# A new prologue, one run of squares and a packed router product in an eight-layer attention kernel with a mixture of experts

## The reference

```
q, k, v = x Wq + bq, x Wk + bk, x Wv + bv
Q, K    = elu(q) + 1, elu(k) + 1
KV, Ks  = sum over the sequence of K*v, of K
V       = Q * KV / (Q * Ks + 1e-6)
x       = layernorm(gelu(V Wo + bo) + x)
x       = layernorm(gelu(gelu(x Wf1 + bf1) Wf2 + bf2) + x)
```

## Time and profile before

| | before |
|---|---|
| median of 3 runs | 1018.92 us (1017.19 to 1019.16) |
| profiled execution | 1018.27 us |
| its span | 1016.2 us |
| PE busy | 952.5 us, 94% |
| DVE busy | 883.3 us, 87% |
| ACT busy | 823.2 us, 81% |
| POOL busy | 108.2 us, 11% |

### The profile page before, as it was taken

The page is one execution under the profiler, slowest core; times in us unless marked ns, Lnnn a source line. Parts: engine busy times, 40 slices in busy tenths (PEclk is TensorE's granted clock), DMA queues, the critical chain, the costliest instruction groups (busy, mean ns, idle before and its releaser), DMA issues.

```text
span 1016.2 us, 13426 instructions
## 1 busy us (share of the span) xinstructions
PE 952.5 (94%) x3621; PEld 606.3 (60%) x3621; DVE 883.3 (87%) x2332; ACT 823.2 (81%) x1334; POOL 108.2 (11%) x109
## 2 busy tenths in 40 slices
PE   5799999999999999999999999999999889999994
PEld 3555555555555555555555555555555567777773
DVE  6768999999999999999999999999998787788875
ACT  4689999999999999999899999999998754444442
POOL 3100000000000000000000000000001122333331
PEclk9999999999999999999999999999999999999997
DMA  9000000000000000020000000000002000000000
GB/s 338 1 0 1 1 0 1 1 1 1 0 1 1 1 0 1 1 83 1 1 1 6 1 1 1 0 1 1 1 0 83 1 1 1 11 11 12 12 21 21
DMA packets 8200, 15.86 MB, mean 16 GB/s; under 512 B 960, under 2 KB 5440, under 8 KB 8000
## 3 DMA queue, kind: packets, MB, share of 16 engines
q1 hardware_dynamic: 7696, 14.82, 4.1%
q10 hardware_dynamic: 432, 0.20, 0.1%
HBM read 12.92 MB, written 2.10 MB: 15 GB/s over the span
## 4 chain that ended last, share of the span: by engine, by line
PE 60%; ACT 15%; DVE 13%; issue 10%; POOL 1%; DMA 1%; SPq 0%; POOLq 0%; DVEq 0%; ACTq 0%
PE Oa L866 11%; PE Ob L866 7%; PE R L764 7%; PE R L766 6%; PE R L765 6%; PE SV L907 4%; ACT L609 4%; PE Ob L821 3%; ACT rs L493 2%; DVE Kt L1425 2%; ACT rz L472 2%; ACT L648 2%; DVE rz L1357 2%; PE Cb L821 1%; PE Ca L886 1%
## 5 line engine op out<-in xcount | busy, mean ns | idle before, releaser
L512 ACT ACTIVATE hid<-R,par 128x512 f32<-128x512 f32 x224 | 148.5, 698 | 14.2 <-PE R L766 12.2
L866 PE MATMUL Oa<-hid,wraw 128*128 128x512 f32 x256 | 133.7, 603 | 1.4
L866 PE MATMUL Ob<-hid,wraw 128*128 128x512 f32 x256 | 130.8, 592 | 0.0
L764 PE MATMUL R<-x_h,wf_h 128*128 128x512 f32 x224 | 105.7, 472 | 0.5 <-ACT hid L512 0.5
L764 PE MATMUL R<-xr_h,wqkv_h 128*128 128x512 f32 x160 | 87.5, 547 | 14.5 <-DVE cen L1685 10.4
L493 ACT ACTIVATE rs<-SV,eps_ln 128x512 f32<-128x512 f32 x128 | 88.4, 690 | 11.7 <-PE SV L907 6.4
L1272 DVE SCALAR_TENSOR_TENSOR y<-x,par,y 128x512 f32<-128x512 f32 x120 | 87.5, 749 | 3.9 <-ACT y L521 3.6
L1283 DVE TENSOR_TENSOR y_l<-y,y_h 128x512 fp32r<-128x512 f32 x128 | 87.8, 686 | 1.2
L765 PE MATMUL R<-x_l,wf_h 128*128 128x512 f32 x224 | 87.9, 392 | 0.0
L766 PE MATMUL R<-x_h,wf_l 128*128 128x512 f32 x224 | 87.9, 392 | 0.0
L498 ACT ACTIVATE rs<-rs 128x512 f32<-128x512 f32 x128 | 80.8, 631 | 1.2
(11 more groups left out here) (249 smaller groups left out, 2400.1 us busy)
## 6 DMA issues: line engine op xcount, KB each, us to landing
wraw<-w_dram SPq DMA_DIRECT2D x7, 768.0 KB, 12.1
x<-x_dram SPq DMA_DIRECT2D x8, 256.0 KB, 6.0
Q<-x_dram SPq DMA_DIRECT2D x1, 2048.0 KB, 7.3
out_dram<-reluq SPq DMA_DIRECT2D x7, 256.0 KB, 2.3
wraw<-w_dram SPq DMA_DIRECT2D x2, 512.0 KB, 5.2
wraw<-w_dram SPq DMA_DIRECT2D x1, 576.0 KB, 6.5
wraw<-row_dram SPq DMA_DIRECT2D x1, 512.0 KB, 5.0
wraw<-bias_dram SPq DMA_DIRECT2D x1, 512.0 KB, 6.1
```

Source lines behind the costliest of these rows:

```text
L512: nc.scalar.activation(hid[:, m * CH:(m + 1) * CH], HIDDEN[m][:, :], GELU, bias=param(u // 4, BF1 + m % FB)).then_inc(hid_done, 1)
L764: nc.tensor.matmul(bank, w_h, a_h, start=True, stop=False)
L866: mm = nc.tensor.matmul(O[h][:, :], raw(u // 4, WF2 + j * P, P), hid[:, m * CH:(m + 1) * CH], start=(j == 0), stop=(j == FB - 1))
```

## The change

It does six things.

1. **Order and banks of the first step.** The prologue becomes a `first_step` on PE, DVE and ACT. K and V of units 0 and 1 come ahead of Q; V alternates between R1 and SV, Q between Oa and Ca, so that each has its own bank. Q's parts of unit 1 lie in `hid`, unused yet. Unit 2's K, V and its first Q are in this step too; its second Q is in step 1; unit 3 moves from step 1 to step 2.
2. **Row copies on three engines.** DVE makes the high part of chunk 0 and the low parts of 0 to 3 and 6, 7; ACT the high parts of 1 to 7 (`split_first`, in step 1 for 6 and 7) and of Wf1; POOL the low parts of 4 and 5 alone.
3. **PE's start.** PE no longer waits for `cen`, whose copy moves behind the first four halves. Ahead of its first product stand 44 unread products of `mean_r` with itself (128x128), into Ob. The fill of 15, and those of 14 in steps 0 and 1, become one of 14 in step 0.
4. **A table load** for exp and log follows the two gelus of step 0 at once.
5. **Router.** The high and low parts of the router weight lie side by side (`rw_parts`): two passes a tile in place of three, 8 and 4 columns wide. DVE adds the two halves with one more reduction, so a chunk's gates have 20 operations (19 before).
6. **Squares.** `squares` of tile 2 and `scale_x` run one after the other, not woven.

On DVE, at the start of the program (xr_h and xr_l are the parts of a chunk, R0 to R2 and SV banks, Kt the product K*V): before,

The diff, cut to its core:

```diff
-            if s < 2:
-                return s + 2
-            return s + 1 if 3 <= s < UNITS - 1 else None
+            return s + 1 if 1 <= s < UNITS - 1 else None
+
+        def q_bank(u, h):
+
+            return (O[0], CB[0])[h] if u < 2 else Q_BANK[h]
+
+        def v_bank(u, h):
+            return (R[1], SV)[h] if u < 2 else V_BANK
+
+        def q_parts(u, h):
+
+            if u == 1:
+                return hid[:, half(h)], hid[:, half(2 + h)]
+            return expq[:, half(h)], reluq[:, half(h)]
...
+            def split_first(c):
+
+                u, h = c // 2, c % 2
+                act.wait_ge(x_loaded[c], 16)
+                after(act, Q_mm, upto(u - 2, h))
+                nc.scalar.activation(xr_h[:, ring(u, h)], x[:, chunk(u, h)], ACT.Copy).then_inc(first_high, 1)
+
+            def high_f_first():
+                act.wait_ge(wfirst_loaded, 16)
+                nc.scalar.activation(wf1_h[0][:, :], raw(0, WF1, FB * P), ACT.Copy).then_inc(wf_high, 1)
+
+            def first_step():
+                exp_k(0, 0)
+                exp_k(0, 1)
+                exp_q(0, 0)
+                relu_q(0, 0)
+                exp_k(1, 0)
+                exp_q(0, 1)
+                relu_q(0, 1)
+                split_first(4)
+                exp_k(1, 1)
+                split_first(5)
+                for h in range(2):
+                    exp_q(1, h)
+                    relu_q(1, h)
+                high_f_first()
+                exp_k(2, 0)
+                exp_k(2, 1)
+                log_z(0)
+                exp_z(0)
+                nc.scalar.preload_act_table_set("gelu_apprx_tanh_and_others")
+                gelu_attend(0, 0)
+                gelu_attend(0, 1)
+                nc.scalar.preload_act_table_set("natural_log_exp_and_others")
+                square(0, 0, 0)
+                high_square(0, 0, 0)
+                square(0, 0, 1)
...
+                if s == 1:
+                    log_z(1)
                 if attends and s % 2 == 1:
                     exp_z(s)
+                if s == 1:
+                    split_first(6)
+                    split_first(7)
...
-            for u in range(2):
-                for h in range(2):
-                    exp_k(u, h)
-                    exp_q(u, h)
-                    relu_q(u, h)
+            for c in range(1, 4):
+                split_first(c)
...
-                    nc.tensor.matmul(SV[:, 0:QKV], cen[:, :], w[:, 0:QKV], start=True, stop=True)
+                    nc.tensor.matmul(O[1][:, 0:w.shape[1]], mean_r[:, :], w, start=True, stop=True)
...
-                    o = O[0][:, t * EXPERTS:(t + 1) * EXPERTS]
-                    nc.tensor.matmul(o, xe_h[:, par_tile(k, t)], rw_h[:, :], start=True, stop=False)
-                    nc.tensor.matmul(o, xe_l[:, par_tile(k, t)], rw_h[:, :], start=False, stop=False)
-                    mm = nc.tensor.matmul(o, xe_h[:, par_tile(k, t)], rw_l[:, :], start=False, stop=True)
+                    both = O[0][:, 2 * t * EXPERTS:2 * (t + 1) * EXPERTS]
+                    nc.tensor.matmul(both, xe_h[:, par_tile(k, t)], rw_parts[:, :], start=True, stop=False)
+                    mm = nc.tensor.matmul(both[:, 0:EXPERTS], xe_l[:, par_tile(k, t)], rw_h, start=False, stop=True)
...
+            def first_step():
+                pe.wait_ge(consts_set, 2)
+                fill(44, mean_r[:, :])
+                for h in range(2):
+                    project(-1, 0, h, "K")
+                    project(-1, 0, h, "V")
+                for h in range(2):
+                    project(-1, 0, h, "Q")
+                    project(-1, 1, h, "K")
+                    project(-1, 1, h, "V")
+                for h in range(2):
+                    project(-1, 1, h, "Q")
+                project(1, 2, 0, "K")
+                project(1, 2, 0, "V")
+                project(1, 2, 1, "K")
+                pe.wait_ge(sums_done, 2)
+                fill(14, wqkv_h[0][:, :])
+                attend_out(0, 0, None)
+                attend_out(0, 1, None)
+                project(1, 2, 1, "V")
+                project(1, 2, 0, "Q")
+                pe.wait_ge(consts_set, 4)
+                pe.wait_ge(reluq_done, upto(1, 1))
+                centre(0, 0, 0)
+                centre(0, 0, 1)
...
-                if s == 0:
-                    fill(15, wqkv_h[0])
                 if p is not None:
                     project(s, p, 1, "Q")
+                if p is not None and s > 1:
                     project(s, p, 1, "V")
...
-                if s == 1:
-                    pe.wait_ge(ln_done[0], upto(0, 1))
-                    pe.wait_ge(wf_set, 1)
-                    fill(14, wf1_h[0])
...
-                if s == 0:
-                    fill(14, wqkv_h[0])
...
+            def high_first():
+
+                dve.wait_ge(x_loaded[0], 16)
+                nc.vector.tensor_copy(xr_h[:, ring(0, 0)], x[:, chunk(0, 0)]).then_inc(chunk0_high, 1)
+
+            def low_first(c):
                 u, h = c // 2, c % 2
-                dve.wait_ge(x_loaded[c], 16)
-                after(dve, kvq_mm, 3 * upto(u - 2, h))
-                nc.vector.tensor_copy(xr_h[:, ring(u, h)], x[:, chunk(u, h)]).then_inc(first_high, 1)
+                if c == 0:
+                    dve.wait_ge(chunk0_high, 1)
+                else:
+                    dve.wait_ge(first_high, c)
+                nc.vector.tensor_tensor(xr_l[:, ring(u, h)], x[:, chunk(u, h)], xr_h[:, ring(u, h)].bitcast(F32),
+                                        ALU.subtract).then_inc(first_low, 1)
...
-                count(nc.vector.tensor_tensor(by_tile(logits[:, :]), by_tile(O[0][:, 0:TE]),
+                parts = O[0][:, 0:2 * TE].rearrange("p (t j e) -> p t e j", t=TILES, j=2)
+                count(nc.vector.tensor_reduce(by_tile(logits[:, :]), parts, AX.X, ALU.add))
+                yield
+                previous()
+                count(nc.vector.tensor_tensor(by_tile(logits[:, :]), by_tile(logits[:, :]),
...
+            def first_step():
+
+                def project(u, h):
+                    min_k(u, h)
+                    make_k(u, h)
+                    k_by_v(u, h)
+
+                split_qkv_first()
+                high_first()
+                for c in range(4):
+                    low_first(c)
+                dve.wait_ge(par_loaded, 16)
+                nc.vector.tensor_scalar(bias1[:, :], par[:, :], 1.0, None, ALU.add).then_inc(consts_set, 1)
+                dve.wait_ge(consts_set, 3)
+                for u in range(2):
+                    for h in range(2):
+                        project(u, h)
+                sums(1)
+                min_q(0, 0)
+                min_q(0, 1)
+                make_q(0, 0)
+                make_q(0, 1)
+                dve.wait_ge(consts_loaded, 32)
+                nc.vector.tensor_copy(cen[:, :], consts[:, P:2 * P]).then_inc(consts_set, 1)
+                low_f_first()
+                project(2, 0)
+                attend(0, 0)
+                attend(0, 1)
+                min_q(1, 0)
+                make_q(1, 0)
+                sum_y(0, 0, 0)
+                high_y(0, 0, 0)
+                low_y(0, 0, 0)
+                sum_y(0, 0, 1)
+                high_y(0, 0, 1)
+                low_y(0, 0, 1)
+                min_k(2, 1)
+                low_square(0, 0, 0)
+                make_k(2, 1)
+                k_by_v(2, 1)
+                min_q(1, 1)
+                make_q(1, 1)
...
+                if s == 1:
+                    low_first(6)
+                    low_first(7)
...
-            split_qkv_first()
-            split_first(0)
-            split_first(1)
-            dve.wait_ge(par_loaded, 16)
-            nc.vector.tensor_scalar(bias1[:, :], par[:, :], 1.0, None, ALU.add).then_inc(consts_set, 1)
-            split_first(2)
-            split_first(3)
-            dve.wait_ge(consts_loaded, 32)
-            nc.vector.tensor_copy(cen[:, :], consts[:, P:2 * P]).then_inc(consts_set, 1)
-            dve.wait_ge(consts_set, 4)
-            for u in range(2):
-                for h in range(2):
-                    min_k(u, h)
-                    make_k(u, h)
-                    k_by_v(u, h)
-                    if u % 2 == 1 and h == 1:
-                        sums(u)
-                    min_q(u, h)
-                    make_q(u, h)
-                    split_first(2 * u + h + 4)
-            split_f_first()
...
-                weave(squares(it, k, 2) if routes else none, scale_x(it, k + 1) if enters else none)
+                if routes:
+                    weave(squares(it, k, 2))
+                if enters:
+                    weave(scale_x(it, k + 1))
                 if routes:
                     weave(squares(it, k, 3))
-                weave(itertools.islice(gating, 7))
+                weave(itertools.islice(gating, 8))
...
-            for c in range(8):
-                low_first(c)
+            low_first(4)
+            low_first(5)
```

(6 more changed lines are left out.)

125 lines of the change are left out of this document (70 added, 55 removed).

## The result

| | before | after |
|---|---|---|
| median of the runs beside each other | 1018.08 us (1017.19 to 1019.16, 4 runs) | 1008.78 us (1007.73 to 1010.24, 4 runs) |
| profiled execution, its span | 1018.27, 1016.2 us | 1008.5, 1006.7 us |
| PE busy | 952.5 us, 94% | 954.6 us, 95% |
| DVE busy | 883.3 us, 87% | 888.4 us, 88% |
| ACT busy | 823.2 us, 81% | 825.6 us, 82% |

The changed kernel is faster: the ratio is 0.9908, with a 95% interval of 0.9892 to 0.9923. That is 9.3 us by the medians and 9.5 by the spans, where 17.4 was forecast; the time lies 0.8 us above the range. The direction was right, the gain about half of the forecast.

The account below looks back on a forecast made before the run. No engine was full early on, so a chain over engines set the time; experts had `gram` waits. Gains of 10.6 us by step 2's end and 6.8 in the experts, 17.4, gave 1001.5 us by the median, range 995 to 1008.

Parts of the forecast that it names:

- The rivals at 1005 to 1008: Slow 44 products 1005 (0.12), halves held up 1006.5 (0.10), no gain in the experts 1008 (0.11).
- 21 in 4.4 us and 23 in 2.6, over at 8.2: PE's start: unread products at the doubled router pace, then the high clock; 0.2 us lost, ends -0.2 to +3.7.
- The first rival: PE's start: the 44 products end at 11.7 or later, the four halves start 3.7 us late; 1005 us, chance 0.12.
- From gelu to the end of step 1 ... I take 10.4: Step 1: 10.4 us where it was 11.4, since V of unit 1 is there before the gelus.
- I take 1.2 a step: Experts: each step gains 1.2 us from squares in one run and a shorter router; 6.8 us in all, ends 1 and 8.5.
- The second rival: Experts give nothing: DVE or ACT's relu replaces the wait, or the strided reduction is dear; 1008 us, chance 0.11.
- the halves of 2.0 us: First step, DVE: four halves of K and V with separate banks, 2.0 us each, 8.0 us from 9.7 to 17.7.
- the rival of the halves: Late Q delays ACT's exp, DVE waits each half; 3 us lost there, 2 in step 1: 1006.5 us, chance 0.10.
- the two hits by POOL: Start, about 14 to 19 us: POOL's operations delay DVE's min_k and min_q, two of about 0.9, 1.8 us.
- unit 3 in step 2: Moving unit 3 into step 2 makes that step 24.3 us for 21.5, giving 2.8 us back.
- the step without `gram`'s wait: Experts: `gram` 3 starts 1.16 us earlier, no wait for Kt above 0.3 us.
- no slower clock through step 2: Against the rival that PE stays at the low clock through steps 1 and 2: 1021.5 us, chance 0.03.

Follow-up runs that it names:

- fills put back: 11 unread 384-column products in step 1 of the changed kernel, 1008.86 us; 26 in PE's waits on the kernel with 20 products, old router, std first, 1001.97 us.
- The best version: Changed kernel with 20 unread products, old router, std split earlier, POOL's layer 1 weight copies held back: 1000.38 us; plus 26 products 1000.13; 11 wide for the 20, 1000.42.
- the old router: Changed kernel with the router's three passes a tile and 19 gate operations, the first from PSUM, as before: 1008.92 us.
- the copies held back: GpSimd's layer 1 weight copies held until unit 0's halves are in the feed part, on the kernel with 20 products, old router, std first: 1000.38 us.
- the second trace with them: 11 unread 512-column products for the 20 of 128, on the kernel with old router, std first and POOL's weight copies held back: 1000.42 us.

## Why the prediction was wrong

| step | forecast | measured | gain lost |
|---|---|---|---|
| first min_k of DVE | 9.7 | 13.12 | 3.4 |
| from there to V of unit 0 | 15.1 | 15.3 | 0.2 |
| V to the first gelu of step 1 | 17.5 | 17.5 | 0 |
| gelu to step 2's table load | 10.4 | 11.9 | 1.5 |
| step 2 | 24.3 | 23.7 | -0.6 |
| experts, gain | 6.8 | 3.4 | 3.4 |

Together 7.9 us: a gain of 9.5 in place of 17.4. The measured times are those of one profile; of the six with this start it had the shortest way to V and to the gelu, so that the two agreements, 15.3 for 15.1 and 17.5 for 17.5, are in part luck (up to 16.4 and 18.3 in the others). From min_k to step 2's table load, 43.0 us by the forecast, they read 43.8 to 46.3. The rivals at 1005 to 1008 were each priced alone, and the range with them: here the first came true, the second by half and the gelu's 1.5 us besides, and together they lie outside.

*The 44 products, the term "21 in 4.4 us and 23 in 2.6, over at 8.2".* The size of one was right: 0.22 us at the low clock. What failed is the clock. I carried over the 4.4 us after which it had risen before, when the passes were 512 columns wide; under passes of 128 it did not rise in 9.65 us, in this trace and in the five others with the same 44. The first min_k came 3.6 us after the 9.5 that I had without the products, near the upper end of 3.7, which I had worked out from another case (0.37 us a pass at the low clock); with 20 in place of 44 the term came out at 9.72. The first rival named this loss (over at 11.7 or later, 1005) at 0.12; alone it would have left the time in the range. The Trainium skill, "TensorE: Matmul & The Clock Gate", section "Wait — 56ns, not 53.3ns?", which gives 107 ns for 128 columns cold, was further off than the rows: a pass here took twice that. Each has its own weight load; that this is what doubles it is not tested.

*"From gelu to the end of step 1 ... I take 10.4".* It is 10.2 where the clock is up, and was 11.9 in this execution, shown by fourteen profiles that fall into two groups. I had weighed the fill that was taken away for `hidden`, and set its cost at nothing since ACT is not ready; the low clock came later than I looked, at the attention output, where ACT does wait. That the removed fill is the cause is not shown: fills put back did not help.

*The experts, "I take 1.2 a step".* The wait for Kt went, 1.16 us, and the four passes' 0.44 as well; but of the 1.2 only 0.57 was left. The sum is closed by the wait that took its place: 0.57 and 0.65 make 1.22. I wrote that the added reduction "stands in the gates, at the head of the chain that turns std" and priced it at its own 0.2; the chain came to be on the path once the squares were 1.2 us earlier, and the same 1.2 us moved it beside POOL's operation, of which it had been clear. I had applied the port rule at 14 to 19 us, where it came out to 0.1 us, and not here. The second rival, "DVE, or ACT's relu, takes the place of the wait", was half true, at 0.11.

*Right:* the halves of 2.0 us for the first two (2.00 and 2.08 from min_k to min_k; the third took 2.56, of it 0.48 of waiting for ACT's exp, as the rival of the halves had it in part), the two hits by POOL, unit 3 in step 2, the step without `gram`'s wait, no slower clock through step 2, and the sign. The best version, 1000.1 to 1000.4 us, beats both kernels by mending two of the three missed terms: fewer unread products and std ahead of the gates; they also have the old router and the copies held back.

## What to carry to other kernels

When a wait of 1 us is removed, follow the chain that ends next as carefully as the wait itself, and ask of each small VectorE operation on it what GpSimd does at its new time: size does not protect it. Unread products ahead of real ones must be over when the first operand is there, and count with their weight load at the low clock. Where the clock of a thin stretch is a term, take it from several profiled executions of the same program, since its place moves.

## What the runs showed of the hardware that was not expected

- 44 passes of 128 columns with their weight loads, 9.65 us without a gap, left TensorE at its low clock in six traces; behind 11 passes of 512 columns in 5.06 us it was at the high one, 0.24 us a pass from 6.5 us on, and likewise in the second trace with them.
- A 128x16 operation of VectorE with both inputs in SBUF took 1.07 us beside a GpSimd operation, and 0.17 with that cut to 0.20 us; the same size with one input in PSUM took 0.17 beside GpSimd.
- Of programs alike up to the experts, one had its low-clock stretch at 36 to 43 us, one from 46.6 us on, and two had two stretches, at 31 to 35 and 48 to 52 us, in their profiled executions. At the start the passes came to the high clock's distance at 12.8 to 15.2 us in these.
